# A graph network kernel: TensorE makes one of the eight tiles of every table chunk of layer 0, and the table is split in bf16 parts as soon as it is stored

## What is computed

```python
h = relu(layernorm(x));  x = x + L0(h, src, dst)
h = relu(layernorm(x));  x = x + L1(h, src, dst, edge_attr_4, edge_attr_32)

def L0(features, src, dst, weight, bias):
    h = features * rsqrt(max(deg_out, 1))[:, None]
    agg = segment_sum(h[src], dst) * rsqrt(max(deg_in, 1))[:, None]
    return relu(agg @ weight + bias)
```

## Time and profile before

| | us |
|---|---|
| median of 3 runs | 4112.62 (4111.1 to 4114.67) |
| span of the profiled execution | 4118.7 |
| first stage of layer 0, from the first one-hot to the last early unit | 318.6 to 883.3 |
| second stage of layer 0, to about | 1978 |
| layer 1 | the rest |

### The profile page before, as it was taken

One profiled execution on the slowest core, in us unless ns is written; L12 is line 12 of the kernel. 1 busy time (PEld: TensorE's weight loads), 2 busy tenths in 40 slices (PEclk: granted clock), 3 DMA queues, 4 the chain that ended last, 5 costly groups with the idle time before them and its releaser, 6 DMA issues.

```text
span 4118.7 us, 83555 instructions
## 1 busy us (share of the span) xinstructions
PE 3138.8 (76%) x20394; PEld 2301.4 (56%) x20395; DVE 2597.2 (63%) x5759; ACT 1927.9 (47%) x6691; POOL 3083.5 (75%) x3210
## 2 busy tenths in 40 slices
PE   5654444467777787777788888888888888888887
PEld 4544444444444443333576667666677667676676
DVE  8994333355555554454577777777777777777776
ACT  3214444443333333333655555555555555555554
POOL 7767777777777777777677777777777777777775
PEclk9996555578888888988899999999999999999998
DMA  2021111111111111111111111111111111111111
GB/s 56 14 53 40 39 39 39 39 28 23 22 23 23 23 22 21 22 22 21 27 29 29 29 29 29 28 29 30 28 28 29 29 30 29 28 28 28 30 28 18
DMA packets 244963, 119.58 MB, mean 29 GB/s; under 512 B 148880, under 2 KB 226065, under 8 KB 244817
## 3 DMA queue, kind: packets, MB, share of 16 engines
q0 software_dynamic: 102528, 52.70, 9.1%
q1 hardware_dynamic: 131625, 48.99, 5.2%
q10 hardware_dynamic: 10768, 17.44, 1.3%
HBM read 113.94 MB, written 4.92 MB: 29 GB/s over the span
## 4 chain that ended last, share of the span: by engine, by line
POOL 58%; issue 24%; DVE 9%; PE 4%; ACT 2%; DMA 2%; DVEq 2%; POOLq 1%; ACTq 0%; SPq 0%
POOL g L447 58%; DVE acc_b L970 4%; DMA g<-table,idx 1%; PE ps L756 1%; PE ps L722 1%; PE ps L790 1%; ACT onehot L554 1%; ACT acc_b L636 1%; DVEq L970 0%; DVE prod_a L1084 0%; ACT onehot L561 0%; DVE prod_a L1075 0%; DVE hn L1228 0%; DVEq L1039 0%; DVEq L1038 0%
## 5 line engine op out<-in xcount | busy, mean ns | idle before, releaser
L447 POOL DMA_INDIRECT g<-table,idx x2980 | 2868.1, 962 | 937.0 <-issue 901.4
L554 ACT ACTIVATE onehot<-iota_all,dst_rel 128x68 f32<-128x68 f32 x3320 | 845.6, 337 | 737.1 <-DVEq L1150 644.4
L846 PE MATMUL ps<-w_s,hid 128*128 128x256 f32 x3328 | 890.5, 419 | 269.2 <-ACT hid L645 221.1
L846 PEld LDWEIGHTS ps<-w_s,hid 128*128 128x128 f32 x3328 | 664.8, 208 | 438.1 <-DVE prod_a L1286 226.9
L657 ACT ACTIVATE q<-g,sh 128x32 f32<-128x32 f32 x1664 | 375.5, 308 | 867.7 <-DMA g<-table,idx 867.7
L756 PE MATMUL ps<-split_s,prod_a 128*128 128x512 bf16 x1736 | 573.9, 415 | 33.1 <-DVE prod_a L1075 31.8
L1291 DVE TENSOR_REDUCE msg_b<-prod_b 128x128 f32<-128x1024 f32 x416 | 502.9, 1209 | 0.0
L722 PE MATMUL ps<-onehot,g 128*33 128x68 f32 x2880 | 267.9, 262 | 286.5 <-issue 222.5
L1261 DVE TENSOR_TENSOR vsh<-g,sh 128x192 f32<-128x192 f32 x208 | 81.7, 393 | 587.1 <-ACT q L660 583.4
L722 PEld LDWEIGHTS ps<-onehot,prod_a 128*128 128x128 f32 x3328 | 388.8, 192 | 86.0 <-issue 85.9
L722 PEld LDWEIGHTS ps<-onehot,g 128*33 128x33 f32 x2880 | 232.1, 136 | 356.8 <-issue 330.4
(11 more groups left out here) (132 smaller groups left out, 3141.3 us busy)
## 6 DMA issues: line engine op xcount, KB each, us to landing
g<-table,idx POOLq DMA_INDIRECT x2980
ef<-edge_t SPq DMA_DIRECT2D x208, 128.0 KB
ef<-src_rows ACTq DMA_DIRECT2D x27, 512.0 KB
prod_a<-src_rows SPq DMA_DIRECT2D x124, 64.0 KB, 3.0
idx<-src_chunks SPq DMA_DIRECT2D x416, 4.0 KB
g<-x_rows,idx POOLq DMA_INDIRECT x224
sh<-sh_chunks SPq DMA_DIRECT2D x208, 16.0 KB
table<-hn ACTq DMA_DIRECT2D x5, 320.0 KB, 3.5
```

The source lines that it names most:

```text
L447: pool.indirect_dma_start(out=g[:, j, t, 0:FEAT], out_offset=None, in_=table, in_offset=bass.IndirectOffsetOnAxis(ap=idx[:, j, t:t + 1], a ...
L554: ins = act.activation(onehot[:, b, t, :], iota_all[:, 0:WIN], ACT.Square, scale=-1.0, bias=dst_rel[:, bass.ds(c * TILES + t, 1)])
L846: mm = pe.matmul(w_ps[h][:, t, :], hid[:, h, P * t:P * t + P], w2_s[:, :], start=True, stop=True)
```

## The change

Every table chunk of layer 0 is gathered with 7 tiles, and TensorE makes the eighth in the first stage too. So the split comes ahead of all units:

- VectorE no longer clears `acc_a` (L1001). ScalarE does, once VectorE has copied the targets that lay there (`dst_taken`).
- ScalarE casts the high parts of the table's 7 blocks, VectorE subtracts them, ScalarE casts the middle parts, VectorE subtracts them into the third part (`split_table`); TensorE's first row sum follows block by block. `split_piece` goes.
- In each table unit VectorE makes the source of the chunk after next and chooses the row of the next chunk; TensorE runs the row sum of the next chunk ahead of its take.
- 56 chunks lose one gather each. SP loads a key row for each of them; the first four key loads stand between the store of the bounds and their reading back.

```diff
-M_ALL = RING * (REG_ITERS - A_ITERS)
+M_ALL = RING * REG_ITERS
@@ SP
             for k in range(2):
                 sp.dma_start(bounds[k:k + 1, :].rearrange("a (q s) -> (a q) s", s=2), mm_c[:, k, :]).then_inc(bounds_out, 16)
+            for j in range(RING):
+                load_key(EARLY + j, j)
             sp.wait_ge(bounds_out, 32)
@@ GpSimd
-            gather(EARLY_ITERS, table1, EARLY_ITERS, kept_four_before)
+            gather(EARLY_ITERS, table1, EARLY_ITERS, kept_four_before, MADE)
...
-            with pool.Fori(0, A_ITERS - 1) as i:
-                gather(i, table1, i + (EARLY_ITERS + 1), beside(i))
-            gather(A_ITERS - 1, table1, A_ITERS + EARLY_ITERS, beside(A_ITERS - 1), taken(True))
+            with pool.Fori(0, A_ITERS) as i:
+                gather(i, table1, i + (EARLY_ITERS + 1), beside(i), MADE)
@@ ScalarE
+            act.wait_ge(zero_made, 2)
+            act.wait_ge(dst_taken, 1)
+            act.activation(acc_a[:, :], zero[:, :].to_broadcast([P, ACC_W]), ACT.Copy).then_inc(acc_a_clear, 1)
+            act.wait_ge(whole_in, 32)
+            for k in range(GROUPS):
+                act.activation(split[0][:, k, :], whole[:, k, :], ACT.Copy).then_inc(highs_made, 1)
+            for k in range(GROUPS):
+                act.wait_ge(high_taken, k + 1)
+                act.activation(split[1][:, k, :], whole[:, k, :], ACT.Copy).then_inc(middles_made, 1)
@@ TensorE
                 for k in range(GROUPS):
+                    if isinstance(m, int) and m == 0:
+                        pe.wait_ge(split_ready, k + 1)
                     for n in range(3):
...
                     else:
+                        source_rows(number(i, k) + 1, (k + 1) % 2)
                         if UNITS[(pos + 1) % len(UNITS)][0]:
                             early_norms(2 * i + UNITS[pos + 1][1])
-                        pe.wait_ge(gathered[k], landed1(i, False))
+                        pe.wait_ge(gathered[k], landed1(i))
+                        pe.wait_ge(row_made, number(i, k) + 1)
                         take(n, RING * i + (EARLY + k), k, pos % 2, lambda t: g[:, k, t, :])
...
-            pe.wait_ge(acc_a_clear, 1)
+            source_rows(0, 0)
             beside_early(0)
@@ VectorE
-            dve.memset(acc_a[:, :], 0.0).then_inc(acc_a_clear, 1)
+            dve.sem_inc(dst_taken, 1)
...
+            def split_table():
+
+                for k in range(GROUPS):
+                    dve.wait_ge(highs_made, k + 1)
+                    dve.tensor_tensor(whole[:, k, :], whole[:, k, :], split[0][:, k, :],
+                                      ALU.subtract).then_inc(high_taken, 1)
+                for k in range(GROUPS):
+                    dve.wait_ge(middles_made, k + 1)
+                    dve.tensor_tensor(split[2][:, k, :], whole[:, k, :], split[1][:, k, :],
+                                      ALU.subtract).then_inc(split_ready, 1)
+
+            def beside_early(i):
 
                 for pos, (is_early, k) in enumerate(UNITS):
+                    if not is_early:
+                        make_source_after_next(i, k)
...
                     if nxt_early:
                         early_onehots(2 * i + nxt_k)
                     if is_early:
                         early_rows(2 * i + k)
+                    else:
+                        choose_next(i, k)
                     take(len(UNITS) * i + pos, 2 * i + k if is_early else RING * i + (EARLY + k), pos % 2)
...
             make_onehot(EARLY, 0, onehot1_ready)
+            make_source(0, 0, 0, 0)
+            make_source(1, 1, 1, 0)
+            split_table()
+            choose(0, EARLY, 0, 0)
+            dve.wait_ge(acc_a_clear, 1)
             beside_early(0)
```

More of the change, by code:

```diff
@@ L56 @@
 LOOK = 1
-FIRST_ROWS = 2
 N_PARAMS = 8 + RING
@@ L307, in gnn_program, with landed1 @@
         GATH = 16 * TILES
[L309 to L317 removed]
+        def landed1(i):
+            return 16 * MADE * i + (GATH * EARLY_ITERS + 16 * MADE)
         def landed2(i):
[L320 removed]
+            return GATH * i + (landed1(REG_ITERS - 1) + GATH)
         def number(i, j):
[L324 removed]
+            return RING * i + j
         w_ps = [ps[:, W_BANK + 2 * b:W_BANK + 2 * b + 2, :].rearrange("p b (u w) -> p (b u) w", w=256)
@@ L360, in load_key, with load1 @@
                 sp.dma_start(keys[:, j, :], row.to_broadcast([P, P])).then_inc(keys_in[j], 16)
-            def load1(i, alone):
+            def load1(i):
                 for j in range(RING):
-                    sp.wait_ge(gathered[j], landed1(i, alone))
+                    sp.wait_ge(gathered[j], landed1(i))
                     sp.dma_start(idx[:, j, :], load_from(src_chunks, RING * i + (EARLY + RING + j))).then_inc(idx_in[j], 16)
-                    if alone:
-                        sp.wait_ge(key_ready, number(i, j) + 1)
-                        load_key(RING * i + (EARLY + RING + j), j)
+                    sp.wait_ge(key_ready, number(i, j) + 1)
+                    load_key(RING * i + (EARLY + RING + j), j)
             def load_from(dram, c):
@@ L392, in _ @@
                 "(p b) f -> p (b f)", b=GROUP)).then_inc(whole_in, 16)
+            with sp.Fori(0, REG_ITERS - 1) as i:
+                load1(i)
             for j in range(RING):
-                load_key(EARLY + RING * A_ITERS + j, j)
-            with sp.Fori(0, A_ITERS) as i:
-                load1(i, False)
-            with sp.Fori(A_ITERS, REG_ITERS - 1) as i:
-                load1(i, True)
-            for j in range(RING):
-                sp.wait_ge(gathered[j], landed1(REG_ITERS - 1, True))
+                sp.wait_ge(gathered[j], landed1(REG_ITERS - 1))
                 sp.dma_start(idx[:, j, :], src_chunks[j]).then_inc(idx_in[j], 16)
@@ L758, in source_rows @@
                 mm.then_inc(rows_psum, 1)
-            def beside_early(i, last=False):
+            def beside_early(i):
                 for pos, (is_early, k) in enumerate(UNITS):
                     n = len(UNITS) * i + pos
-                    if last and pos == FIRST_ROWS:
-                        source_rows(0, 0)
                     if is_early:
@@ L776, in alone @@
                     source_rows(number(i, j) + 1, (j + 1) % 2)
-                    pe.wait_ge(gathered[j], landed1(i, True))
+                    pe.wait_ge(gathered[j], landed1(i))
                     pe.wait_ge(row_made, number(i, j) + 1)
@@ L792, in mid_block @@
                 mm.then_inc(mid_ready, 1)
-            pe.wait_ge(acc_a_clear, 1)
+            source_rows(0, 0)
             beside_early(0)
-            with pe.Fori(1, A_ITERS - 1) as i:
+            with pe.Fori(1, A_ITERS) as i:
                 beside_early(i)
-            pe.wait_ge(split_ready, 1)
-            beside_early(A_ITERS - 1, True)
             pe.wait_ge(par_loaded, 16 * N_PARAMS)
@@ L1150, in take, with beside_early @@
                 dve.sem_inc(joined1, 1)
-            def split_piece(n):
-                here = slice(n * PIECE, (n + 1) * PIECE) if isinstance(n, int) else bass.ds(n * PIECE, PIECE)
-                full, high, middle, rest = (t.rearrange("p k w -> p (k w)")[:, here] for t in (whole, *split))
-                dve.tensor_copy(high, full).then_inc(split_chain, 1)
-                dve.wait_ge(split_chain, 3 * n + 1)
-                dve.tensor_tensor(full, full, high, ALU.subtract).then_inc(split_chain, 1)
-                dve.wait_ge(split_chain, 3 * n + 2)
-                dve.sem_inc(split_step, 1)
-                dve.tensor_copy(middle, full).then_inc(split_chain, 1)
-                dve.wait_ge(split_chain, 3 * n + 3)
-                ins = dve.tensor_tensor(rest, full, middle, ALU.subtract)
-                if isinstance(n, int) and n == A_ITERS - 1:
-                    ins.then_inc(split_ready, 1)
-            def beside_early(i, last=False):
-                for pos, (is_early, k) in enumerate(UNITS):
-                    if last and pos == 0:
-                        make_source(0, 0, 0, 0)
-                        make_source(1, 1, 1, 0)
-                    if last and pos == FIRST_ROWS + 1:
-                        choose(0, RING * A_ITERS + EARLY, 0, 0)
+            def split_table():
[7 more added lines that the diff above has]
+                                      ALU.subtract).then_inc(split_ready, 1)
+            def beside_early(i):
+                for pos, (is_early, k) in enumerate(UNITS):
+                    if not is_early:
+                        make_source_after_next(i, k)
                     nxt_i, nxt_pos = (i, pos + 1) if pos + 1 < len(UNITS) else (i + 1, 0)
@@ L1184, in alone @@
                 for j in range(RING):
-                    next_rows(i, j)
+                    make_source_after_next(i, j)
+                    choose_next(i, j)
                     if j == LOOK:
```

36 lines of the change are left out of this document (9 added, 27 removed).

## The result

| | before | changed |
|---|---|---|
| median of 4 runs each, us | 4111.86 (4109.72 to 4114.67) | 4223.06 (4221.55 to 4223.58) |
| ratio, with its 95% interval | | 1.0269 (1.0257 to 1.0281) |
| span of the profiled execution, us | 4118.7 | 4221.5 |
| end of the first addition of layer 0 | 322.28 | 336.72 |
| end of the last addition of the first stage | 883.33 | 997.25 |

The changed kernel is **2.7% slower** (111 us; 4245 was forecast, 4190 to 4300). The two profiled executions differ by 102.8 us: 14.4 in the opening, 99.5 in the first stage, 4.9 given back in the second, and 6.2 less in layer 1, where the program does not differ.

What follows compares the result with a forecast made beforehand. GpSimd bounds the first stage before, the VectorE-TensorE chain after: 24.5 us per half, 49.8 per iteration, 698 for fourteen. Stage end +144 us, 12 given back, net +132 on 4118.7, less 6.1 for the median: 4245 us, range 4190 to 4300.

Steps and rivals of the forecast that it cites:

- Which engine bounds the stage: First stage of layer 0: GpSimd bounds it before; after, VectorE and TensorE take 49.8 us per iteration against GpSimd's 35.8.
- (a): First table unit of a half iteration: VectorE's choice waits for TensorE's row sum, 8.84 us in all.
- (b): Second table unit, on VectorE alone: source 2.06, one-hots 3.71, choice to addition 3.15, gaps 0.27, sum 9.19 us.
- (c): Early unit, unchanged: VectorE picks the norms, TensorE takes, VectorE adds, 6.51 us.
- The loop's turn: Once per iteration of the first stage: an issue gap of 1.89 instead of 1.13 us, added to two half iterations.
- The opening: Before the first stage: first addition of layer 0 ends at 339 instead of 322.28 us.
- What the second stage gives back: GpSimd enters with up to three chunks more in the ring: 12 us back, bounds 0 and 27.
- The clock: TensorE's granted clock in the first stage would be 0.8 or more, against 0.53 before.
- low-clock rival: TensorE never rises in the first stage: row sums 8.9 us, stage 910 us, kernel about 4461 us; chance 0.06.
- What the ramp costs in each half: TensorE's slower row sum and take after a gap in the first stage: about 2.1 us per half, 59 in all.
- VectorE hiding the rest: First stage: TensorE's parts lie wholly behind VectorE's, 38.3 us an iteration, kernel 4095 us; chance 0.05.
- GpSimd staying the bound: First stage: all 72 us of removed gathers come in, kernel 4041 us; chance 0.02.

Runs made afterwards that it cites:

- c1: Changed kernel with VectorE's choice for the second table unit moved into the early unit, behind the early rows: 4175.86 us, ratio 1.0161 to the kernel before.
- x1: Changed kernel with TensorE's row sum for the first table unit moved ahead of the early unit's take: 4100.91 us, ratio 0.9977 to the kernel before.
- s1: Kernel before with only the changed opening, still 8 gathers per chunk: 6169.78 us on a slower chip, ratio 0.9947 to the kernel before.
- g8_kept_third: Changed kernel with the first stage's eighth gather kept, into an unread spare tile; third run: 6316.59 us on a slower chip, ratio 1.0106 to the kernel before.
- x2: Changed kernel with both the choice moved into the early unit and the row sum ahead of the early take: 4082.26 us, ratio 0.9930 to the kernel before.

## Why the prediction was right, point by point

**Which engine bounds the stage: right, and shown.** GpSimd waits 179.5 us for one-hots in the first stage (over 100 was named), and c1 and x1 move the time by moving VectorE's and TensorE's instructions past each other while every gather stays. That the saved gathers are worth nothing in the changed kernel itself was not shown by a run; it is argued from those waits and from an iteration of 47.8 us against the 41.0 that GpSimd would need with all of them.

**(a) The first table unit: 8.84 predicted, 8.84 measured.** One passage in the trace of before carried it. x1 shows that 3.88 us of it are the place of the row sum. That it came out to the hundredth is partly luck: the others, from the third iteration on, take 8.76 to 8.86 us.

**(b) The second table unit: 9.19 predicted, 8.47 measured. This is the term that was mis-sized.** The price of the source (2.06 us from the addition's end) was taken from the one place where the stage changes; in the loop it is 1.75 (623.85 to 625.60). The one-hots are 3.61 instead of 3.71, choice to addition 3.11 instead of 3.15, and the gaps of 0.27 are none: VectorE's instructions start up to 0.1 us before the end of the one ahead. 28 x 0.72 = 20 us.

**(c) The early unit: 6.51 predicted, 6.58 measured.**

**The loop's turn: 0.76 predicted for an iteration, next to none measured (8.84 against 8.82 us).** This term was wrong in kind. The gap is there (0.79 instead of 0.37 us ahead of L1066, so 0.42 and not 0.76), but the choice behind it waits 3.12 instead of 3.77: the row sum hides it. I had added a gap on VectorE ahead of a wait for TensorE, which a walk over both engines would have dropped. Fourteen times 0.76 is 11 us. With the 20 us of (b) and 2 of the opening, less 2 that (c) took longer, these are the 31 us by which the stage ended before 1028. x1 confirms the reading, since the turn costs 0.46 us again where the choice no longer waits.

**The opening: 339 predicted, 336.7 measured.** The shift started at 304.45 (304 chosen between 299 and 309.8). The subtractions were 0.63 instead of 0.70 us, and the row sum was over at 329.0 instead of 329.5. From there to the first addition's end 9.2 us were predicted, as from an early unit on, and 7.7 measured: the choice there waits 1.12 us for its row sum and not 3.6, since TensorE is at the high level already and does not stop. The price of the opening alone was only argued, since s1 has no run on a chip of 4110 us.

**What the second stage gives back: 12 us predicted, 4.9 measured,** inside the bounds of 0 and 27. GpSimd waits 23.6 us for slots there instead of 5.5: most of the lead of three chunks was spent waiting. The choice of 12 between the bounds had no row behind it.

**The sum.** 14.4 + 99.5 - 4.9 = 109.0 us in layer 0, against 16.4 + 128 - 12 = 132. The walk was about 30 us too long (28.5 in the stage, 2 in the opening), and 7 us too much were given back: the two errors partly cancel, so the 22 us between 4245 and 4223 are smaller than what was mis-sized. The 6.2 us of layer 1 are a difference between two executions (its 1664 gathers last 957 ns in the mean before and 954 after, 5 us in all); the medians differ by 111.2.

**The clock: right.** 0.86 was granted in the stage (0.8 or more was named), so the low-clock rival was out (4461 in the prediction; its own terms, 910 us for the stage against 698, give 4457). What the ramp costs in each half is (5.99 - 4.65) + (2.02 - 1.14) = 2.2 us by rows at either level, 62 us in all, 1.5% of the span. The prediction's terms for it, 1.23 and 1.01, add up to 2.24 us and 63 in all, not 2.1 and 59; its sum does not use that total. The Trainium skill ("TensorE: Matmul & The Clock Gate", Part 1) has a ramp under 1% of a typical kernel's span. This kernel is not typical in that, since its trace shows the ramp with each of 28 gaps; held to 1%, the forecast would have come nearer to the result (by 18 us in the prediction's words, by 22 with the sum put right), but for a reason that the rows don't bear out.

**The other rivals.** VectorE hiding the rest (4095) would have needed an iteration under 39.5 us; x1 has 38.85 and comes to 4100.91. That is near what the rival priced (38.3), but not by its mechanism: VectorE still waits 2.59 us for the take in each half of x1, and its own terms were priced too high ((b) above, and 5.43 us for a first table unit of 4.96). GpSimd staying the bound (4041) never came near. The rule of the Trainium skill ("DMA: Bandwidth & Descriptors", the section on the SWDGE path), an estimate of 2.04 us for each gather, does not hold between gathers here: they start 0.967 + 0.29 = 1.26 us apart in the changed kernel too.

## What to carry to other kernels

When work moves from the bounding engine to two others, walk one turn of the loop over both of them, unit by unit, and add a term only if nothing is waiting behind it: the issue gap at the loop's turn lay ahead of a wait and cost nothing. Work that needs nothing of the unit it stands behind belongs into the gap in which its engine waits; here one such move was worth more than the whole change had cost, partly because the gap it filled had let TensorE's clock fall. A change that loses 2.7% as written can win 0.7% with its instructions in another order, so read which wait ends last before giving it up.

## What the runs showed of the hardware that was not expected

- Some chips run the same program in 6.2 ms instead of 4.1 ms. The instructions of VectorE and table gathers last the same there (an addition 220 instead of 218 ns, a gather 950 instead of 958, g8_kept_third against the changed kernel); the waits for another engine's or a transfer's signal are what grows (1977 instead of 372 us ahead of the additions, most of it ended by "remote"; GpSimd waits 1021 us for its indices). TensorE's matmuls do last longer in the mean (the 256-column ones 477 instead of 420 ns), with a mean granted clock of 0.77 instead of 0.92. No kernel but the one before was run on both kinds of chip; but g8, which only adds gathers to the changed kernel, stands at 1.008 to 1.011 there, where the changed kernel alone stands at 1.027. So experiments that are compared must share the chip, and a chip of the kind that the question is about. What makes these chips slower stays open.
- Small differences go with a level of the clock: in x2 a gap of 1.55 us ahead of the norms left the take behind them at 1.14 us, one of 1.76 us came with a take of 2.02, in nearly every iteration. The length of the gap does not decide it: in x1 gaps of 1.75 and 1.76 us ahead of the norms (649.63 and 688.57 us) were followed by takes of 1.14. What does decide it stays open.
- From the end of the VectorE instruction that frees it to its first matmul, the early take needs 1.24 us in the changed kernel (635.19 to 636.43) and 1.23 in x1 (637.96 to 639.19), more than the take itself at the high level.
